# Attention scores in 32-row tiles over four PSUM banks, with v, k's transpose and z in the same banks

## The reference

```
x = x + 0.5 * ffn(layernorm(x))           # FP4-quantized gate, up, down
x = x + attn(layernorm(x))                # 16 heads of 16 features
x = x + 0.5 * ffn(layernorm(x))

attn: qkv = x @ Wqkv.T + bqkv
      q = (elu(q) + 1 + 1e-4) / 4;  k = elu(k) + 1 + 1e-4
      num = q . cumsum(k v);  den = q . cumsum(k) + 1e-4   # causal, per head
      out = (num / den) @ Wout.T + bout
      layernorm(out) * gamma + beta
```

## Time and profile before

| | |
|---|---|
| three runs, median (lowest to highest) | 2425.37 us (2424.32 to 2426.82) |
| the profiled execution's own time | 2427.61 us |
| its span, first to last instruction | 2425.9 us |
| busy over the span: PE, DVE, POOL, ACT | 93%, 89%, 83%, 75% |
| mean granted TensorE clock | 0.976 of full speed |
| v's copies into v_eo's layout, issue to landing | 1.9 us, 512 DMAs |
| transposes by DMA of x and o in the attention, issue to landing | 2.4 us, 128 each |

### The profile page before, as it was taken

One profiled execution on the slowest core, in us unless ns is written; L12 is line 12 of the kernel. 1 busy time (PEld: TensorE's weight loads), 2 busy tenths in 40 slices (PEclk: granted clock), 3 DMA queues, 4 the chain that ended last, 5 costly groups with the idle time before them and its releaser, 6 DMA issues. The chain is left out here.

```text
span 2425.9 us, 75807 instructions
## 1 busy us (share of the span) xinstructions
PE 2244.2 (93%) x22786; PEld 1632.9 (67%) x22786; DVE 2166.5 (89%) x5377; ACT 1825.2 (75%) x3782; POOL 2022.5 (83%) x3234
## 2 busy tenths in 40 slices
PE   1499999999999289999999999996899999999998
PEld 1266666666666189999999999996466666666665
DVE  7499999999999469999999999997899999999997
ACT  2588888888887167777777777775888888888885
POOL 0499999999998179999999999986799999999996
PEclk9799999999999699999999999998999999999999
DMA  1265555555555223232332323232455555555555
GB/s 36 69 117 115 116 113 115 113 113 113 113 112 91 44 56 64 62 63 62 63 63 63 63 62 64 62 64 41 75 114 113 113 113 111 113 113 113 111 114 115
DMA packets 730325, 215.33 MB, mean 89 GB/s; under 512 B 661657, under 2 KB 730009, under 8 KB 730268
## 3 DMA queue, kind: packets, MB, share of 16 engines
q1 hardware_dynamic: 730268, 214.65, 43.3%
HBM read 20.52 MB, written 16.78 MB: 15 GB/s over the span
## 5 line engine op out<-in xcount | busy, mean ns | idle before, releaser
L577 PE MATMUL ffn_ps_gu<-wgu_hi,ffn_xT 128*128 128x512 f16 (+1 forms) x3072 | 738.0, 363 | 49.8 <-DMA ffn_xT<-ffn_x_hl 49.8
L577 PEld LDWEIGHTS ffn_ps_gu<-wgu_hi,ffn_xT 128*128 128x128 f16 x3072 | 301.1, 98 | 335.7 <-DMA ffn_xT<-ffn_x_hl 52.1
L577 PE MATMUL ffn_ps_gu<-wgu_lo,ffn_xT 128*128 128x512 f16 (+1 forms) x1536 | 431.5, 363 | 0.0
L531 ACT ACTIVATE ffn_quarter<-ffn_y,offsets 128x960 int16<-128x960 f32 (+2 forms) x264 | 282.9, 1072 | 184.7 <-DVE ffn_y L467 184.1
L587 PE MATMUL ffn_ps_down<-wd_hi,ffn_hT 128*128 128x256 f16 x2816 | 350.4, 273 | 23.9 <-DVE x_sb L456 14.7
L512 POOL TENSOR_TENSOR ffn_h_hl<-ffn_q,ffn_h_scale_hi 128x704 f16<-128x704 f16 x256 | 351.4, 1373 | 15.9 <-DVE ffn_h_scale_lo L473 13.1
L513 POOL TENSOR_TENSOR ffn_h_hl<-ffn_q,ffn_h_scale_lo 128x704 f16<-128x704 f16 x256 | 354.2, 1384 | 0.0
L587 PEld LDWEIGHTS ffn_ps_down<-wd_hi,ffn_hT 128*128 128x128 f16 x2816 | 264.5, 98 | 106.1 <-issue 37.5
L436 DVE TENSOR_REDUCE ffn_per_block<-ffn_hx 128x60 f32<-128x960 f32 (+2 forms) x264 | 298.5, 1131 | 41.7 <-ACT ffn_hx L561 19.3
L467 DVE TENSOR_TENSOR ffn_y<-ffn_hx,ffn_per_block 128x960 f32<-128x960 f32 (+2 forms) x264 | 295.3, 1119 | 0.0
L559 ACT ACTIVATE ffn_odd<-ffn_quarter,offsets 128x960 f16<-128x960 int16 (+2 forms) x264 | 278.7, 1056 | 0.0
(11 more groups left out here) (203 smaller groups left out, 5731.4 us busy)
## 6 DMA issues: line engine op xcount, KB each, us to landing
attn_v_eo<-attn_v_nat SPq DMA_DIRECT2D x512, 34.0 KB, 1.9
x_sb<-in_L_attn_x SPq DMA_DIRECT2D x128, 128.0 KB, 2.3
out<-x_sb SPq DMA_DIRECT2D x128, 128.0 KB, 2.1
ffn_xT<-ffn_x_hl SPq DMA_TRANSPOSE x256, 2.4
ffn_hT<-ffn_h_hl SPq DMA_TRANSPOSE x256, 3.6
attn_xT<-attn_x_hl SPq DMA_TRANSPOSE x128, 2.4
attn_oT<-attn_o_hl SPq DMA_TRANSPOSE x128, 2.4
raw_qkvo<-in_L_attn_Wqkv SPq DMA_DIRECT2D x1, 768.0 KB
```

Of the source, the lines that this page charges most:

```text
L531: nc.scalar.activation(quarter[:, back], y[:, back], ACT.Identity, bias=offsets[:, 0:1], scale=4.0 / HALF_MIN).then_inc(S["quarter"], 1)
L577: last = nc.tensor.matmul(ps_gu[par][:, a:b], xT[par][:, c, :], w[:, k, a:b], start=(n == 0), stop=(n == len(terms) - 1))
```

## The change

The score matmul takes 32 feature rows r (one pair of heads) instead of 64, so that no other pair has to be masked out of q: q_feat itself is the moving operand, `q_rows` and its two mask vectors go, with three instructions of the set-up. Each call has 64 stationary columns (one parity a) and 64 moving columns, so there are 32 of them, and row tile r writes its own PSUM bank. `ps_sc` now has four banks of which scores fill one half; the other halves hold v, k's transpose and z. TensorE's step becomes: q and k(i+1), transpose of k(i), z(i-3), v(i+1), num(i-1), scores(i), kv(i), and scores wait until the three neighbours are read. `zg` gets a second buffer, z comes one tile later than before, and BEHIND is 5.

VectorE's step, the instructions as before, becomes: statistics of x (i+4), x_sb plus zg times z_rstd (i-5, was i-4), aggregate of x (i+4), before(i), statistics of z (i-3), features (i+1), v_nat(i+1), aggregate of z (i-3), zg(i-3), den, rden and o (i-1), masked scores(i), first(i), second(i). On ScalarE k_nat(i) moves behind the exp of tile i+1. On POOL the two z_rstd instructions come one tile later.

```diff
-        AHEAD, BEHIND = 4, 4
+        AHEAD, BEHIND = 4, 5
-        scores = sb("scores", [P, 2, DC, 2, 2, SUB])
+        scores = sb("scores", [P, PAIRS, DC, 2, SUB])
-        zg = sb("zg", [P, D])
-        ps_kT_v = psum("ps_kT_v", [P, 512])
-        ps_z = psum("ps_z", [P, 512])
-        ps_sc = psum("ps_sc", [P, 2, DC, 2, 2, SUB])
+        zg = pair("zg", [P, D])
+        ps_sc = psum("ps_sc", [P, PAIRS, 2, DC * 2 * SUB])
+        def four(r):
+            return slice(r * 2 * E, (r + 1) * 2 * E)
+        ps_of_scores = ps_sc[:, :, 0, :].rearrange("p r (m q) -> p r m q", q=SUB)
+        ps_v, ps_kT, ps_z = [ps_sc[:, r, 1, :] for r in range(3)]
...
 -                    nc.vector.tensor_tensor(scores[:].rearrange("p g c s j q -> p (g c s j) q"), ps_sc[:].rearrange("p g c s j q -> p (g c s j) q"),
-                                            causal[:].unsqueeze(1).to_broadcast([P, 4 * PAIRS, SUB]), ALU.mult).then_inc(S["masked"], 1)
+                    nc.vector.tensor_tensor(scores[:].rearrange("p r c s q -> p r (c s) q"), ps_of_scores,
+                                            causal[:].unsqueeze(1).unsqueeze(1).to_broadcast([P, PAIRS, DC * 2, SUB]), ALU.mult).then_inc(S["masked"], 1)
...
 -                    for j in range(2):
-                        last = nc.scalar.activation(q_rows[par][:, :, j, :], expo[par][:, 0:DC, :], ACT.Identity, bias=of_pair_eps[:, j:j + 1], scale=of_pair[:, j:j + 1])
-                    last.then_inc(S["q_rows"], 1)
...
 +                    ready(pe, "feat", i)
+                    freed(pe, "masked", i, 1)
+                    for c in range(DC):
+                        last = nc.tensor.transpose(ps_kT[:, c * P:(c + 1) * P], expo[par][:, DC + c, :], ident[:])
+                    last.then_inc(S["kT_done"], 1)
+                if valid(to, N):
+                    turned(pe, "oT", to, oth)
+                    freed(pe, "z_gamma", to, 1)
+                    nc.tensor.matmul(ps_z, ones3[:], bout3[:], start=True, stop=False)
...
                      ready(pe, "k_odd", i)
-                    ready(pe, "q_rows", i)
-                    freed(pe, "masked", i, 1)
+                    ready(pe, "q_feat", i)
+                    ready(pe, "k_nat", i)
+                    if valid(tf, N):
+                        ready(pe, "v_nat", tf)
+                    if valid(to, N):
+                        ready(pe, "z_gamma", to)
                     for c in range(DC):
                         for s in range(2):
-                            for g in range(2):
-                                last = nc.tensor.matmul(ps_sc[:, g, c, s], k_eo[par][half(g), c, s], q_rows[par][half(g), c, :, half(s)], start=True, stop=True)
+                            for a in range(2):
+                                for r in range(PAIRS):
+                                    last = nc.tensor.matmul(ps_sc[half(a), r, 0, (c * 2 + s) * SUB:(c * 2 + s + 1) * SUB], k_eo[par][four(r), c, s, a], q_feat[par][four(r), c, half(s)],
+                                                            start=True, stop=True)
```

More of the change, by code:

```diff
@@ L593 @@
 ATTN_SEMS = ("sums", "stats", "var", "rstd", "shift", "xn", "x_hi", "x_split", "turn", "xT_even", "xT_odd", "qk_done", "relu", "exp", "feat", "k_even", "k_odd",
-             "q_feat", "q_rows", "v_done", "v_nat", "v_eo_even", "v_eo_odd", "kT_done", "k_nat", "scores_done", "masked", "kv_done", "kv_first", "kv_second",
+             "q_feat", "v_done", "v_nat", "v_eo_even", "v_eo_odd", "kT_done", "k_nat", "scores_done", "masked", "kv_done", "kv_first", "kv_second",
              "mid", "before", "num_done", "den", "rden", "o_ready", "o_hi", "o_split", "oT_even", "oT_odd", "proj_done",
@@ L745, in step @@
                 oth = 1 - par
[L746 to L752, removed]
+                ts, tf, tm, tz, ta = i + 4, i + 1, i - 1, i - 3, i - 5
                 if valid(ts, N):
@@ L757, in step @@
                     nc.vector.bn_stats(bn6[:], x_sb[:, ts, :]).then_inc(S["sums"], 1)
-                if valid(tz, N):
-                    ready(dve, "z_sums", tz)
+                if valid(ts, N):
+                    ready(dve, "sums", ts)
                 if valid(ta, N):
@@ L763, in step @@
                     ready(dve, "z_gamma", ta)
-                    nc.vector.scalar_tensor_tensor(x_sb[:, ta, :], zg[:], z_rstd[par][:], x_sb[:, ta, :], ALU.mult, ALU.add).then_inc(attn_added, 1)
-                if valid(tz, N):
-                    nc.vector.bn_aggr(z_mv[oth][:], z_bn6[:]).then_inc(S["z_stats"], 1)
-                if valid(ts, N):
-                    ready(dve, "sums", ts)
+                    nc.vector.scalar_tensor_tensor(x_sb[:, ta, :], zg[oth][:], z_rstd[oth][:], x_sb[:, ta, :], ALU.mult, ALU.add).then_inc(attn_added, 1)
+                if valid(ts, N):
+                    nc.vector.bn_aggr(mv[par][:], bn6[:]).then_inc(S["stats"], 1)
+                if valid(i, N) and not (isinstance(i, int) and i == 0):
+                    ready(dve, "mid", tm)
+                    ready(dve, "kv_second", tm)
+                    freed(dve, "num_done", i, 2)
+                    nc.vector.scalar_tensor_tensor(before[par][:], mid[oth][:], column(keep, i), second[:], ALU.mult, ALU.add).then_inc(S["before"], 1)
+                if valid(tz, N):
+                    ready(dve, "proj_done", tz)
+                    freed(dve, "z_stats", tz, 1)
+                    freed(dve, "z_rstd", tz, 2)
+                    nc.vector.bn_stats(z_bn6[:], ps_z).then_inc(S["z_sums"], 1)
+                if valid(tf, N):
+                    ready(dve, "exp", tf)
+                    nc.vector.scalar_tensor_tensor(expo[oth][:], ps_qk[:], unscale[:, 0:1], expo[oth][:], ALU.mult, ALU.max).then_inc(S["feat"], 1)
+                if valid(tz, N):
+                    ready(dve, "z_sums", tz)
                 if valid(tf, N):
@@ L774, in step @@
                         placed(dve, tf - 2, oth)
+                if valid(tf, N):
                     nc.vector.scalar_tensor_tensor(v_nat[oth][:].rearrange("p a j w -> p (a j) w")[:, :, 0:E], blocks(ps_v), unscale[:, 0:1], blocks(v_bias[:]),
                                                    ALU.mult, ALU.add).then_inc(S["v_nat"], 1)
-                if valid(ts, N):
-                    nc.vector.bn_aggr(mv[par][:], bn6[:]).then_inc(S["stats"], 1)
                 if valid(tz, N):
+                    nc.vector.bn_aggr(z_mv[oth][:], z_bn6[:]).then_inc(S["z_stats"], 1)
                     ready(dve, "z_stats", tz)
[L782 to L792, removed]
+                    nc.vector.scalar_tensor_tensor(zg[oth][:], ps_z, z_mv[oth][:, 0:1], rows[:, 1, :], ALU.subtract, ALU.mult).then_inc(S["z_gamma"], 1)
                 if valid(tm, N):
@@ L884, in step @@
                 if valid(i, N):
[L886 to L889, removed]
                     ready(act, "feat", i)
@@ L893, in step @@
                     nc.scalar.activation(q_feat[par][:], expo[par][:, 0:DC, :], ACT.Identity, bias=feat_eps[:]).then_inc(S["q_feat"], 1)
-                    for j in range(2):
-                        last = nc.scalar.activation(q_rows[par][:, :, j, :], expo[par][:, 0:DC, :], ACT.Identity, bias=of_pair_eps[:, j:j + 1], scale=of_pair[:, j:j + 1])
-                    last.then_inc(S["q_rows"], 1)
                 if valid(tf, N):
                     ready(act, "qk_done", tf)
-                    freed(act, "q_rows", tf, 2)
+                    freed(act, "q_feat", tf, 2)
                     freed(act, "k_odd", tf, 2)
@@ L905, in step @@
                     nc.scalar.activation(expo[oth][:], expo[oth][:], ACT.Exp, scale=-1.0).then_inc(S["exp"], 1)
+                if valid(i, N):
+                    ready(act, "kT_done", i)
+                    freed(act, "kv_done", i, 1)
+                    nc.scalar.activation(k_nat[:], ps_kT, ACT.Identity, bias=feat_eps[:]).then_inc(S["k_nat"], 1)
                 if valid(tn, N):
@@ L928, in step @@
                 oth = 1 - par
[L929 to L936, removed]
+                tf, tn, to = i + 1, i - 1, i - 3
                 if valid(tf, N):
@@ L947, in step @@
                     last.then_inc(S["qk_done"], 1)
+                if valid(i, N):
+                    ready(pe, "feat", i)
+                    freed(pe, "masked", i, 1)
[5 more added lines that the diff above has]
+                    freed(pe, "z_gamma", to, 1)
+                    if not valid(i, N):
+                        pe.wait_ge(S["masked"], N)
+                    nc.tensor.matmul(ps_z, ones3[:], bout3[:], start=True, stop=False)
+                    z_terms = three_terms(oT[oth], wout_hi, wout_lo)
+                    for n, (aT, w) in enumerate(z_terms):
+                        last = nc.tensor.matmul(ps_z, aT, w, start=False, stop=(n == len(z_terms) - 1))
+                    last.then_inc(S["proj_done"], 1)
                 if valid(tf, N):
                     if valid(i, N):
-                        ready(pe, "k_nat", i)
+                        ready(pe, "v_nat", i)
```

(8 more changed lines are left out.)

24 lines of the change are left out of this document (8 added, 16 removed).

## The result

The changed kernel takes 2472.55 us (median of four runs, 2470.07 to 2474.66) against 2425.32: a ratio of 1.0194, 95% interval 1.0176 to 1.0211, or 47.2 us more. The forecast was 2429 and no measurable change; the time lies in the wide range of 2401 to 2494, but 43.5 us above the forecast and outside the forecast's own range, 2421 to 2436.

The account below looks back on a forecast made before the run. TensorE's own order was taken to set the 6.39 us attention step. 2427.61 + 3.8 for the longer step - 0.5 for set-up = 2430.9, on the median 2428.7, rounded 2429; own range 2421 to 2436, with rivals 2401 to 2494.

Parts of the forecast that it names:

- The chain that it names: Attention step: q and k, relu, exp, features, v, aggregate, zg, release; scores start at 5.08 us, TensorE stands 0.25.
- the ring: Scores hold up kv and the next q and k, for which the next relu waits; this closed chain makes the step 6.42.
- release: Delay from VectorE's end of zg to TensorE's start of scores: taken as 0.12 us; 0.06 would give a 6.36 step.
- X = 0.66: Length of the score block on TensorE in us, with all eight tiles side by side: 0.44 for passes plus additions.
- My additions of 0.05, 0.07 and 0.10: In the score block: a pass for weights not loaded ahead 0.05, eight starts 0.07, change of form to kv 0.10 us.
- The forecast's 3.8: Attention stage: step 6.42 instead of 6.39, 0.03 us over 128 steps, thus 3.8 us more.
- its upper rival: Upper end of the wide range, 2494 us: score calls bound by issue; chance 0.25 together with half overlap.
- The rival that issue binds: Score calls come 0.03 us apart after the wait: block 1.17, step 6.93, 2494 us; chance 0.25 together with half overlap.
- its point of decision of 0.014: Issue time per score call in us from which 32 calls and the other 0.21 pass the tiles' 0.66.
- its 0.03 for all 32 calls: Issue spacing of the score calls after a wait in TensorE's sequencer: 32 x 0.03 = 0.96 us.
- Wait not last: Scores' wait for zg ends 0.25 us earlier, TensorE's order gives 6.17, POOL's 6.20: 24 us less, 2401; chance 0.28.
- one after the other: Score passes on TensorE spaced 0.0275 us for any number of tiles: block 1.92, step 7.68, 2590 us; chance 0.07.

Follow-up runs that it names:

- The run without the wait: Changed kernel with z moved out of the scores' banks into free columns of the state's banks, so kv waits for zg instead of scores: 2432.00 us.
- The best version here: Changed kernel with z out of the scores' banks and VectorE reordered: v_nat before features, z's aggregate between, x's sums awaited by before: 2426.07 us, ratio 1.0001.

## Where the prediction was right and where it was wrong

The chain that it names is there: scores wait for zg in every step, the wait closes the ring, and taking the wait away gives 2432. Point by point, measured against forecast:
- q and k 1.52 (1.51); relu 1.78 (1.78), exp's end 3.22 (3.21), v_nat 3.94 (3.91), zg's end 5.02 (4.96), release 0.11 (0.12), scores 5.13 (5.08), kv 0.66 (0.68). TensorE stands 0.30 a step (0.25).
- VectorE was to wait for exp before the features. It has no slack there: features start at 3.29, 0.07 behind exp's end, because VectorE's list reaches them only then. A second ring, from scores over the mask and VectorE's list to the features, is about as long as the one forecast, and VectorE waits for scores instead, 0.2 a step. The 0.05 by which this chain ends later is 6.4 us.
- **The term that failed: X = 0.66.** The score block measured 0.86. The array does what I assumed: eight tiles side by side, passes 0.007 apart, which would be 0.44 for 64; half of them took 0.25. My additions of 0.05, 0.07 and 0.10 make 0.22, and 0.20 lie between the last pass and kv's weights; so their sum is about right, while the parts do not show one by one. What I missed is the stall: behind the 16th call the passes stop for 0.14 and then come at 0.0165 a call, and these other 16 calls took 0.42 instead of 0.22. 0.20 x 128 = 25.6 us.
- **The step that was missing: the loop's turn.** Hidden before (6.39 in every step), it now lies on the ring: 29 turns of 0.36 in the median are some 10.4 us. The run with two steps a turn priced it at 0.32; the one with eight says nothing on it, since the stall there is far larger.

The forecast's 3.8 + 6.4 + 25.6 + 10.4 = 46.2, against 45.3 measured in the stage. These sizes are read from the trace of the changed kernel. The run without the wait (2432.00) and the one with half the calls (2429.69) show that both links belong to the ring, but not what each is worth: both stop at VectorE's own list, 6.42 and 6.43 a step. So by an estimate from these two runs, with this order of VectorE's list the step could hardly fall under 6.42, however short the score block.

That the time lies in the stated range is owed to its upper rival, not to the forecast, which had 0.40 of the chances; slower as a whole had 0.42. The rival that issue binds comes nearest: behind the stall a call takes 0.0165, over its point of decision of 0.014. Its size was wrong, as its 0.03 for all 32 calls left out that the first 16 come at the array's pace. That it is the issue that sets the later pace was not shown. Wait not last and one after the other both fell: TensorE stands in every step, and passes of different tiles start 0.007 apart, not 0.0275.

The change also had less to give than I credited: without any wait its scores take 0.844 against 0.88 before. The best version here, 2426.07, equals the kernel before; none beat it.

## What to carry to other kernels

Before a buffer is shared between stages, add up the ring that its wait closes, and the engine's own list beside it: here the delays on it, a loop's turn too, add up in the step. A block of short calls is not priced by the array's pace alone: here the first 16 calls ran at that pace, the rest behind a stall at a slower one, and the change of form came on top.

## What was not expected of the hardware

- Behind 16 float32 calls of 32x64 the passes stalled for 0.14 us and then came at about 0.0165 us a call, with a wait ahead of the block (0.664 us to the last pass) or without (0.645).
- The change of form behind scores cost 0.20 us from the last pass to the next weights, after 32 passes as after 64. The Trainium skill, TensorEngine Tiling (Array Packing), section Tiling Modes, says that changing the mode drains the engine; the trace agrees.
- The passes of one tile went by its stationary columns: 0.055 us apart at 64, 0.11 at 128, with 64 moving in both.
- One VectorE instruction took 0.53 us at one place and 0.75 to 1.07 in three of four steps at another, where POOL's x_sb and z_rstd ran beside it.
- Eight steps in a loop body instead of four took 75 us more, with six times the instruction packets.
